# First attention of a two-layer hybrid block: heads in halves of eight on two row ranges of the array, scores and exponents issued alternately

## The chip, the cores and the metric

One core of one Trainium2 chip runs the whole program as one launch. The metric is the device time of that launch in microseconds (us), the median over several runs; lower is better.

## The reference, cut to what matters

Four batches of 512 tokens of width 512 go through attention A, a feed-forward layer, attention B and the same feed-forward layer. The change is in attention A, which has 32 heads of width 2 and a mask that keeps 51 keys for each query:

```python
sim = ...                                  # a pairwise network of 512 x 512 tokens
_, top_idx = jax.lax.top_k(sim, 51)        # mask: 0 at these, -inf elsewhere
q, k, v = heads(q), heads(k), heads(v)     # (4, 32, 512, 2)
scores = einsum('bhid,bhjd->bhij', q, k) / sqrt(2) + mask[:, None]
ao = einsum('bhij,bhjd->bhid', softmax(scores), v)
out = x + ao.reshape(B, S, 64) @ Wout.T + bout
```

## The kernel before, in words

The program runs its stages one after another on five queues (TensorE, VectorE, ScalarE, GpSimd, and SyncE for transfers). First comes the pairwise network with its top-k (`pairs`, to about 1055 us), which also projects q and k, splits each into a high and a low half for single-pass matmuls (F32R), and sends them to two stacks `qs` and `ks`. Then attention A (`attention_a`), the feed-forward layer (`feed_forward`), attention B, and the second feed-forward layer.

**The stacks.** A chunk is 16 heads of one batch; there are 8 chunks. A chunk's stack has 112 partitions: three terms (high by high, low by high, high by low) of 32 rows (16 heads by 2), and 16 rows for the negated maxima. `own_keys` is a copy of the chunk's keys in which one head is picked out: GpSimd multiplies `ks` by a column of `own_step` (L1169). It picks by differences, so that the banks need the mask only once per chunk: each further head adds its difference to what stands in PSUM.

**Steps.** `order_of_attention_a` writes out one list of steps. Each step is offered to all five queues, so the list is the order of each queue. The steps are:

- `scores` (c, h, pair): two matmuls (L998) of 128 queries by 512 keys into two of the banks 0 to 3; VectorE takes the maximum of each row over both banks at once (L1085). Banks 0, 1 and banks 2, 3 take turns. 256 steps.
- `place` (c): TensorE turns the chunk's maxima (L1006), ScalarE copies them negated (L1121), SyncE sends them into `qs` (L1185). The chunk's exponents wait for this.
- `exp` (c, keys, h, j): one matmul (L1017) of 128 keys by 512 queries into bank 4 (j = 0) or 5 (j = 1), from which ScalarE makes the exponent (L1129). The matmul waits until ScalarE has read the bank's last content: `pe.wait_ge(ex_made, i - 1)`.
- `weighted` (c, keys, group, j): exponents of four heads by their values, on four column ranges of the array (L1049). It waits for the last of the four exponents.
- At the first head of a chunk the mask is written into the banks first ("seeding"): L996 for scores, L1015 for exponents, bf16 matmuls with the identity.
- Side steps, one at most at each odd step: `turn` (mask transposed, L985), and `divide`, `feature`, `project_a` for a finished batch (L1059, L1066, L1073).
- `last_exp` (h, keys): the exponents of the last chunk, when banks 0 to 3 are free: two matmuls (L1034) and one exponent of both banks (L1135). Beside them run the first steps of the feed-forward layer (`FIRST_ROWS`): normalising rows and turning them (L1449).

`LEAD` = 36 scores steps run before the first exponent; then each exponent step (two `exp`) has one scores step beside it. One head thus needs two scores steps, two exponent steps and one `weighted`; this text calls such a pair of steps a period. TensorE meets in a period: exponent pair, scores pair, scores pair, exponent pair, `weighted`. Its queue is in order, and the wait of a matmul stands on its weight load (PEld).

Of the kernel before, what the change touches and what calls it, by code (L numbers as in the profile page):

```python
# [32 lines left out]
HALVES = 6  # L33
STACK = 16 * (HALVES + 1)

# [38 lines left out]
def build(nc, d):  # L74
    with ExitStack() as ctx:
# [38 lines left out]
        for queue in queues:  # L114
# [3 lines left out]
            queue.wait_ge(p.stacked[0], 16 * 24)  # L118
            queue.wait_ge(p.stacked[1], 16 * 24)
# [72 lines left out]
CHUNK = 16  # L192
CHUNKS = B * HA // CHUNK
LEAD, KEYS_AHEAD = 36, 1
# [44 lines left out]
def order_of_attention_a():  # L239
# [5 lines left out]
    maxima = iter([(c, h, pair) for c in range(CHUNKS) for h in range(CHUNK) for pair in range(2)])  # L245

    def next_maxima():
        for c, h, pair in [at for at in (next(maxima, None),) if at]:
            order.append(("scores", c, h, pair))
            if pair == 0 and CHUNK * c + h + KEYS_AHEAD < CHUNKS * CHUNK:  # L250
                order.append(("own_keys", CHUNK * c + h + KEYS_AHEAD))
            if (h, pair) == (CHUNK - 1, 1):
                places.append(("place", c))

    def place():

        while places and ("scores", places[0][1], CHUNK - 1, 1) not in order[-3:]:
            order.append(places.pop(0))

    for i in range(LEAD):  # L260
        next_maxima()
        place()
    for c in range(CHUNKS - 1):
        b = c // 2
        if c % 2 == 0 and b + 1 < B:
            side += [("turn", b + 1, t) for t in range(NT)]
        for i in range(2 * CHUNK):
            keys, h = divmod(i, CHUNK)
            if h % 2 == 0:
                next_maxima()  # L270
            order += [("exp", c, keys, h, 0), ("exp", c, keys, h, 1)]
            place()
            if h % 2:
                next_maxima()
            if weighted and h % 2 == 0:
                order.append(weighted.pop(0))
                if order[-1][1:] == (c - 1, 1, CHUNK // 4 - 1, 1) and c % 2 == 0:
                    side[:0] = finish_steps(b - 1)
# [4 lines left out]
            if (c % 2, i) == (0, 16) and b + 1 < B:  # L283
                order.append(("values", b + 1))
            if (c, i) == (CHUNKS - 2, 4):
                order.append(("early_root",))
    beside = iter(FIRST_ROWS)
    for h in range(CHUNK):
# [4 lines left out]
        order += next(beside, [])  # L293
        if h % 4 == 3:
            weighted += [("weighted", CHUNKS - 1, keys, h // 4, j) for keys in range(2) for j in range(2)]
# [23 lines left out]
def attention_a_memory(k, mem):  # L319
    a = Core()  # L320
    sb, signal = k.sb, k.flag
    a.ks = sb(mem, "ks", [STACK, B, 2, S])
# [2019 lines left out]
```

## Time and profile before

| | us |
|---|---|
| median of 3 runs | 3141.8 (3140.8 to 9992.69) |
| the profiled execution's own time | 3138.7 |
| its span, first to last instruction | 3137.5 |
| lead of scores alone | 1067.3 to 1116.5 |
| exponents with scores beside them | 1116.5 to 1496.8 |
| last exponents | 1496.8 to 1543.9 |
| TensorE busy / VectorE / ScalarE / GpSimd | 2981.5 / 2335.7 / 1771.8 / 1061.6 |
| mean granted TensorE clock | 0.975 |

The median and the profiled execution differ by 3.1 us. A busy time of TensorE counts the matmul's whole passage, so consecutive matmuls overlap in it; how fast they follow is read from the starts in a timeline. A row of the timeline merges like instructions: its first number is the first one's start, its second the time that they cover. "[0.21 <-ACT ex L1129]" means that the engine stood idle for 0.21 us before it, and what ended that. The clock is a share of 2.4 GHz.

### The profile page before, as it was taken

To read this page: it belongs to the slowest core of one execution; us is meant where nothing else is said; L and a number is where in the kernel's file an instruction comes from. 1 tells how busy PE (TensorE), PEld (TensorE's weight loads), DVE (VectorE), ACT (ScalarE), POOL (GpSimd) and SP (SyncE) were. 2 spreads that over 40 slices of the span, in tenths; PEclk is the share of its full clock that TensorE was granted. 3 is DMA by queue.
4 is the path that set the end of the run, shared out by engine and by line. 5 is a ranking of instruction groups with operands and counts; after the bars stand their busy time and mean duration, and the time that the engine had idled before them with its cause. 6 is when DMAs were issued, how large, how long until landed. Compare 5 with 4: busy or idle time off the path is not lost. (4 is left out here: it accounts for less than half of the span.)

```text
span 3137.5 us, 56845 instructions
## 1 busy us (share of the span) xinstructions
PE 2981.5 (95%) x22569; PEld 1795.1 (57%) x22569; DVE 2335.7 (74%) x4298; ACT 1771.8 (56%) x2897; POOL 1061.6 (34%) x881
## 2 busy tenths in 40 slices
PE   6999999999999799999899999989999987999999
PEld 3545445444556545444478778844444425887787
DVE  6998999999999877777366676655766766667665
ACT  4988888888889356666643333314443443334332
POOL 1000000000000454533255565504544554565653
PEclk9999999999999789999999999999999988999999
DMA  2000000000000000000112111143332311112111
GB/s 76 2 2 12 2 2 12 2 2 12 2 2 2 1 2 1 2 1 1 35 44 58 51 44 51 44 126 96 81 88 77 93 34 54 44 56 72 53 50 49
DMA packets 105805, 112.93 MB, mean 36 GB/s; under 512 B 8963, under 2 KB 74500, under 8 KB 105157
## 3 DMA queue, kind: packets, MB, share of 16 engines
q1 hardware_dynamic: 102918, 108.61, 12.3%
q8 instruction: 180, 2.95, 0.4%
q10 hardware_dynamic: 2624, 0.69, 0.1%
q14 instruction: 83, 0.68, 0.1%
HBM read 84.76 MB, written 20.97 MB: 34 GB/s over the span
## 5 line engine op out<-in xcount | busy, mean ns | idle before, releaser
L734 DVE TENSOR_SCALAR pair_in<-key_words,row_words 128x512 f32<-128x512 f32 x1792 | 725.8, 480 | 33.6 <-PE ps L620 29.6
L819 ACT ACTIVATE pair_mid<-ps,row_bias 128x512 f32<-128x512 f32 x896 | 589.3, 691 | 114.9 <-PE ps L620 97.4
L620 PE MATMUL ps<-pair_in,w_hi 128*32 128x512 f16 x7168 | 625.7, 390 | 11.7 <-DVE pair_in L734 11.3
L620 PE MATMUL ps<-pair_in,w_lo 128*32 128x512 f16 x3584 | 393.3, 390 | 0.0
L1085 DVE TENSOR_REDUCE maxes<-ps 128x2 f32<-128x1024 f32 x256 | 303.4, 1221 | 96.9 <-PE ps L998 95.8
L620 PEld LDWEIGHTS ps<-pair_in,w_hi 128*32 128x32 f16 x7168 | 256.1, 95 | 205.1 <-issue 37.5
L847 POOL TENSOR_SCALAR_AFFINE_SELECT sim<-sim 128x512 f32<-128x512 f32 x16 | 10.2, 641 | 1030.2 <-ACT sim L836 1030.2
L1129 ACT ACTIVATE ex<-ps 128x512 f32<-128x512 f32 x448 | 243.3, 595 | 119.0 <-PE ps L1017 118.4
L1495 PE MATMUL ps<-ffn_b_hi,ffn_a_hi 128*128 128x512 f32 x904 | 286.1, 398 | 25.1 <-DVE ffn_up L1583 9.1
L1495 PE MATMUL ps<-ffn_b_lo,ffn_a_hi 128*128 128x512 f32 x904 | 282.2, 394 | 1.7 <-DVE ffn_b_lo L1565 1.7
L1495 PE MATMUL ps<-ffn_b_hi,ffn_a_lo 128*128 128x512 f32 x904 | 281.2, 393 | 0.7 <-POOL ffn_a_lo L1726 0.7
L1633 DVE TENSOR_TENSOR x<-x,ps 128x512 f32<-128x512 f32 x256 | 175.6, 686 | 136.2 <-PE ps L1512 133.3
L635 PE MATMUL ps<-pair_mid,w_slide 128*32 128x512 f32 x2048 | 247.3, 592 | 0.0
L2240 ACT ACTIVATE ex_b<-ps 128x512 f32<-128x512 f32 x256 | 147.4, 598 | 168.4 <-PE ps L2084 162.3
L2172 DVE TENSOR_REDUCE maxes_b<-ps 128x1 f32<-128x512 f32 x256 | 169.3, 682 | 85.8 <-PE ps L2069 85.3
L1495 PEld LDWEIGHTS ps<-ffn_b_hi,ffn_a_hi 128*128 128x128 f32 x904 | 169.1, 190 | 69.6 <-DVE ffn_up L1583 11.7
L1726 POOL TENSOR_TENSOR ffn_a_lo<-ffn_sums,ffn_a_hi 128x1024 fp32r<-128x1024 f32 x60 | 148.4, 2473 | 171.0 <-ACT ffn_a_hi L1648 171.0
L1693 ACT ACTIVATE ffn_gate<-ffn_gate 128x512 f32<-128x512 f32 x60 | 37.9, 632 | 277.0 <-DVE ffn_gate L1590 277.0
L1495 PEld LDWEIGHTS ps<-ffn_b_lo,ffn_a_hi 128*128 128x128 f32 x904 | 171.4, 190 | 39.8 <-DVE ffn_b_lo L1565 3.6
L1495 PEld LDWEIGHTS ps<-ffn_b_hi,ffn_a_lo 128*128 128x128 f32 x904 | 171.4, 190 | 37.5 <-POOL ffn_a_lo L1726 1.1
L2022 POOL TENSOR_TENSOR ex_sum<-ex_sum,ex_b 128x512 f32<-128x512 f32 x124 | 156.9, 1283 | 81.9 <-ACT ex_b L2240 81.7
L620 PEld LDWEIGHTS ps<-pair_in,w_lo 128*32 128x32 f16 x3584 | 128.6, 95 | 88.2 <-issue 27.6
(240 smaller groups left out, 5434.0 us busy)
## 6 DMA issues: line engine op xcount, KB each, us to landing
ffn_raw_up<-in_w_ffn SPq DMA_DIRECT2D x64, 512.0 KB, 4.0
ffn_raw_down<-in_w_ffn SPq DMA_DIRECT2D x64, 256.0 KB, 2.7
q_stack<-halves SPq DMA_DIRECT2D x48, 256.0 KB, 5.1
k_stack<-halves SPq DMA_DIRECT2D x48, 256.0 KB, 5.9
halves<-hi_b SPq DMA_DIRECT2D x16, 512.0 KB, 2.6
halves<-lo_b SPq DMA_DIRECT2D x16, 512.0 KB, 3.6
out<-x SPq DMA_DIRECT2D x4, 1024.0 KB, 4.4
x<-in_x SPq DMA_DIRECT2D x6, 512.0 KB, 6.1
```

Source lines behind the costliest of these rows:

```text
L620: s = nc.tensor.matmul(ps[32 * quarter:32 * quarter + 32, bank + which, :], w_part[:, at_w:at_w + 32], words.rearrange("p (s two) -> p s t ...
L635: s = nc.tensor.matmul(ps[32 * c:32 * c + 32, 6 + w, :], p.w3_slide[:, 30 - 2 * r:62 - 2 * r], p.pair_mid[:, n % NG, half, :], start=r == ...
L734: s = nc.vector.tensor_scalar(p.pair_in[:, (4 * n + i) % N_PAIR, :], p.key_words[:, b % 2, :], p.row_words[:, b % 2, row:row + 1], None, A ...
L819: nc.scalar.activation(p.pair_mid[:, n % NG, which, :], ps[:, bank + which, :], ACT.Relu, bias=bias).then_inc(p.mid_made, 1)
L1085: nc.vector.tensor_reduce(maxes[:, c % 2, 2 * pair:2 * pair + 2, h], ps[:, 2 * pair:2 * pair + 2, :], AX.X, ALU.max).then_inc(maxes_made, 1)
L1129: nc.scalar.activation(ex[:, i % N_EX, :], ps[:, EXP_BANKS[j], :], ACT.Exp, scale=2.0 ** -0.5).then_inc(ex_made, 1)
L1495: i = nc.tensor.matmul(bank, a_part[:, s % 2, a_at, h, :], b_part[:, place(operand), h, :], start=opens and (which, m, h) == (0, 0, 0), st ...
L1633: nc.vector.tensor_tensor(x[:, n, :], x[:, n, :], ps[:, 6 + t % 2, :], ALU.add).then_inc(x_added, 1)
L1726: nc.gpsimd.tensor_tensor(lo, source, hi.bitcast(F32), ALU.subtract).then_inc(w_lo_made, 1)
L2022: engine.tensor_tensor(ex_sum[:, g, :], first, ex[:, i % N_EX, :], ALU.add).then_inc(done, 1)
L2172: nc.vector.tensor_reduce(maxes[:, n % 2, g, t:t + 1], ps[:, O1_BANKS[i % 3], :], AX.X, ALU.max).then_inc(max_made, 1)
L2240: nc.scalar.activation(ex[:, i % N_EX, :], ps[:, O2_BANKS[i % 2], :], ACT.Exp, scale=SCALE).then_inc(ex_made, 1)
```

## The change

A half-chunk g is now 8 heads; there are 16. A chunk's two halves lie one above the other: the even half on partitions 0 to 55 of `qs`, `ks` and `own_keys`, the odd half on 64 to 119 (48 rows of terms and 8 of maxima each). One GpSimd instruction makes the `own_keys` of a head of both halves at once, so there are 64 instead of 128. The matmuls keep their columns (128 by 512) and contract over 56 rows instead of 112. While the exponents of half g run, the scores are those of half g + 1 (12 steps of 16, on the other row range) or g + 2 (the last 4 steps, on the same row range). A step's four matmuls are issued score, exponent, score, exponent. `weighted` stands ahead of the even step instead of behind its exponents. `LEAD` is 20. The exponents kept are 24 instead of 16. Masks are seeded, and maxima placed, for each half. The last half has 16 `last_exp` steps instead of 32, and a `FIRST_ROWS` entry may follow each one instead of every second. In the pair stage the stacks take 24 transfers a batch instead of 12, and the two stacks are cleared in full at the start.

```diff
-CHUNK = 16
+CHUNK, HEADS = 16, 8
 CHUNKS = B * HA // CHUNK
-LEAD, KEYS_AHEAD = 36, 1
+HALF_CHUNKS = CHUNKS * CHUNK // HEADS
+STACK = TERMS * 2 * HEADS + HEADS
+LEAD, KEYS_AHEAD = 20, 1
...
-    for c in range(CHUNKS - 1):
+    for g in range(HALF_CHUNKS - 1):
...
-        for i in range(2 * CHUNK):
-            keys, h = divmod(i, CHUNK)
-            if h % 2 == 0:
-                next_maxima()
-            order += [("exp", c, keys, h, 0), ("exp", c, keys, h, 1)]
-            place()
-            if h % 2:
-                next_maxima()
+        for i in range(2 * HEADS):
+            keys, h = divmod(i, HEADS)
             if weighted and h % 2 == 0:
                 order.append(weighted.pop(0))
...
+            for j, scores in enumerate(next_maxima()):
+                order += scores[:1] + [("exp", g, keys, h, j)] + scores[1:]
+            place()
             if h % 4 == 3:
-                weighted += [("weighted", c, keys, h // 4, j) for j in range(2)]
+                weighted += [("weighted", c, keys, 2 * half + h // 4, j) for j in range(2)]
...
-    for h in range(CHUNK):
+    for h in range(HEADS):
         for keys in range(2):
             order.append(("last_exp", h, keys))
             if weighted:
                 order.append(weighted.pop(0))
-        order += next(beside, [])
+            order += next(beside, [])
...
+    def own_keys(n, half):
+        return own[64 * half:64 * half + STACK, n % N_KEYS, :]
+
+    def queries(g):
+        return a.qs[64 * (g % 2):64 * (g % 2) + STACK, g // 4, g // 2 % 2, :]
...
         elif kind == "exp":
-            c, keys, h, j = at
-            b, u, n, t, i = c // 2, c % 2, CHUNK * c + h, 2 * keys + j, nth_exp(*at)
-            pe.wait_ge(in_place[c % 2], 16 * (c // 2 + 1))
+            g, keys, h, j = at
+            b, n, t, i = g // 4, HEADS * (g // 2) + h, 2 * keys + j, nth_exp(*at)
+            pe.wait_ge(in_place[g % 2], 16 * (g // 2 + 1))
             pe.wait_ge(ex_made, i - 1)
...
-            nc.tensor.matmul(ps[:, EXP_BANKS[j], :], own_keys(n)[:, t * P:t * P + P], a.qs[:, b, u, :],
+            nc.tensor.matmul(ps[:, EXP_BANKS[j], :], own_keys(n, g % 2)[:, t * P:t * P + P], queries(g),
```

Before, TensorE's queue in the middle of the stage, where the exponent banks are seeded (L998 scores, L1015 seed, L1017 exponents, L1049 weighted; before.py's lines):

```order
L1017 MATMUL ps<-qs,first_keys 128x512 x2
L1049 MATMUL ps<-ex,v_aug 12x512 x4
L1017 MATMUL ps<-qs,first_keys 128x512 x2
L998 MATMUL ps<-more_keys,qs 128x512 x4
L1015 MATMUL ps<-mask_t,ident_bf 128x512
L1017 MATMUL ps<-qs,first_keys 128x512
L1015 MATMUL ps<-mask_t,ident_bf 128x512
L1017 MATMUL ps<-qs,first_keys 128x512
L1049 MATMUL ps<-ex,v_aug 12x512 x4
L1017 MATMUL ps<-qs,first_keys 128x512 x2
L998 MATMUL ps<-more_keys,qs 128x512 x4
L1017 MATMUL ps<-qs,first_keys 128x512 x2
```

Changed, TensorE at such a seeding (L1011 scores, L1029 seed, L1031 exponents, L1061 weighted; after.py's lines):

```order
L1061 MATMUL ps<-ex,v_aug 12x512 x4
L1011 MATMUL ps<-own_keys,qs 128x512
L1029 MATMUL ps<-mask_t,ident_bf 128x512
L1031 MATMUL ps<-qs,own_keys 128x512
L1011 MATMUL ps<-own_keys,qs 128x512
L1029 MATMUL ps<-mask_t,ident_bf 128x512
L1031 MATMUL ps<-qs,own_keys 128x512
L1011 MATMUL ps<-own_keys,qs 128x512
L1031 MATMUL ps<-qs,own_keys 128x512
L1011 MATMUL ps<-own_keys,qs 128x512
L1031 MATMUL ps<-qs,own_keys 128x512
L1061 MATMUL ps<-ex,v_aug 12x512 x4
```

The exponent pair that stood alone behind `weighted` now has a score ahead of each exponent, and a seed stands between a score and an exponent. In the plain periods, on the same engine, it now reads:

```order
L1061 MATMUL ps<-ex,v_aug 12x512 x4
L1011 MATMUL ps<-own_keys,qs 128x512
L1031 MATMUL ps<-qs,own_keys 128x512
L1011 MATMUL ps<-own_keys,qs 128x512
L1031 MATMUL ps<-qs,own_keys 128x512
L1011 MATMUL ps<-own_keys,qs 128x512
L1031 MATMUL ps<-qs,own_keys 128x512
L1011 MATMUL ps<-own_keys,qs 128x512
L1031 MATMUL ps<-qs,own_keys 128x512
L1061 MATMUL ps<-ex,v_aug 12x512 x4
```

The scores no longer stand together between the two exponent pairs, and `weighted` comes directly behind the odd step's second exponent and ahead of a score.

Before, TensorE's queue where the last exponents begin (L1006 turned maxima, L1030 seed, L1034 last exponents, L1449 turned rows of the feed-forward layer):

```order
L1049 MATMUL ps<-ex,v_aug 12x512 x4
L1017 MATMUL ps<-qs,more_keys 128x512 x2
L1030 MATMUL ps<-mask_t,ident_bf 128x512 x2
L1034 MATMUL ps<-qs,first_keys 128x512 x2
L1049 MATMUL ps<-ex,v_aug 12x512 x4
L1030 MATMUL ps<-mask_t,ident_bf 128x512 x2
L1034 MATMUL ps<-qs,first_keys 128x512 x2
L1049 MATMUL ps<-ex,v_aug 12x512 x4
L1034 MATMUL ps<-qs,first_keys 128x512 x8
L1449 MATMUL ps<-ident,ffn_z 128x128 x4
L1034 MATMUL ps<-qs,first_keys 128x512 x4
```

Changed, the same place (L1020, L1041, L1045, L1461 in after.py):

```order
L1020 MATMUL ps<-ident,maxes 8x128 x4
L1061 MATMUL ps<-ex,v_aug 12x512 x4
L1031 MATMUL ps<-qs,own_keys 128x512 x4
L1041 MATMUL ps<-mask_t,ident_bf 128x512 x2
L1045 MATMUL ps<-qs,own_keys 128x512 x2
L1061 MATMUL ps<-ex,v_aug 12x512 x4
L1041 MATMUL ps<-mask_t,ident_bf 128x512 x2
L1045 MATMUL ps<-qs,own_keys 128x512 x2
L1061 MATMUL ps<-ex,v_aug 12x512 x4
L1045 MATMUL ps<-qs,own_keys 128x512 x2
L1461 MATMUL ps<-ident,ffn_z 128x128 x4
```

The turned rows begin after one plain last exponent step instead of four, and from there stand behind every step.

## Rows read from the trace of the kernel before

**Rows 1.** The page, part 1: busy time, share of the span, instructions of each engine.

```profile
PE 2981.5 (95%) x22569; PEld 1795.1 (57%) x22569; DVE 2335.7 (74%) x4298; ACT 1771.8 (56%) x2897; POOL 1061.6 (34%) x881
```

**Rows 2.** Busy time by stretch, us; (x) counts instructions, PEclk is TensorE's granted clock.

```profile
1068.00:1117.00 49.00, 43.57 (x87) 19.38 (x86) 43.17 (x37) 1.87 (x2) 43.28 (x32) 0.53 0.00 1
1117.00:1491.00 374.00, 370.67 (x1926) 183.00 (x1925) 283.49 (x297) 255.37 (x479) 158.73 (x108) 1.00 0.01 1
1500.00:1510.00 10.00, 7.98 (x40) 3.58 (x32) 0.69 (x1) 9.53 (x12) 0.00 (x0) 1.00 0.37 108
```

**Rows 3.** Groups by line, 1117 to 1496.7 us (TensorE's to 1491): count | busy us, mean ns | idle before.

```profile
L1085 DVE TENSOR_REDUCE maxes<-ps 128x2 f32<-128x1024 f32 x220 | 260.6, 1221 | 88.6 <-PE ps L998 87.9
L1129 ACT ACTIVATE ex<-ps 128x512 f32<-128x512 f32 x447 | 242.8, 595 | 119.0 <-PE ps L1017 118.4
L985 PE MATMUL ps<-ident_bf,mask 128*128 128x128 bf16 x48 | 4.8, 222 | 0.0
```

**Rows 4.** Timeline, one period from 1179.69 us: start, us, engine, line, op, out<-in.

```profile
1179.69 0.30 PEld L1017 LDWEIGHTS ps<-qs,more_keys 112*128 112x128 f32 x2 [0.85 <-ACT ex L1129]
1179.69 0.73 PE L1017 MATMUL ps<-qs,more_keys 112*128 112x512 f32 x2
1180.23 1.08 ACT L1129 ACTIVATE ex<-ps 128x512 f32<-128x512 f32 x2 [0.60 <-PE ps L1017]
1180.26 1.08 PE L998 MATMUL ps<-first_keys,qs 112*128 112x512 f32 x4
1181.18 0.68 PE L1017 MATMUL ps<-qs,more_keys 112*128 112x512 f32 x2
1181.36 0.19 PEld L1017 LDWEIGHTS ps<-qs,more_keys 112*128 112x128 f32 x1 [0.22 <-ACT ex L1129]
1181.79 1.05 PE L1049 MATMUL ps<-ex,v_aug 128*12 128x512 f32 x8
1182.77 0.73 PE L1017 MATMUL ps<-qs,more_keys 112*128 112x512 f32 x2
```

**Rows 5.** Timeline, a period in which no scores are left, from 1491.78 us.

```profile
1491.78 1.05 PE L1049 MATMUL ps<-ex,v_aug 128*12 128x512 f32 x8
1493.33 0.60 PE L1006 MATMUL ps<-ident,maxes 128*16 128x128 f32 x4
1493.94 0.98 PE L1017 MATMUL ps<-qs,more_keys 112*128 112x512 f32 x2
1494.43 0.19 PEld L1017 LDWEIGHTS ps<-qs,more_keys 112*128 112x128 f32 x1 [0.30 <-ACT ex L1129]
1494.85 1.05 PE L1049 MATMUL ps<-ex,v_aug 128*12 128x512 f32 x8
```

**Rows 6.** Timeline of TensorE around 1168 us: seeding the two exponent banks.

```profile
1168.36 0.39 PE L1015 MATMUL ps<-mask_t,ident_bf 128*128 128x512 bf16 x1
1168.83 0.39 PE L1015 MATMUL ps<-mask_t,ident_bf 128*128 128x512 bf16 x1
```

**Rows 7.** Timeline of TensorE in the lead of scores alone.

```profile
1104.16 2.26 PE L998 MATMUL ps<-first_keys,qs 112*128 112x512 f32 x4 [0.34 <-DVE maxes L1085]
1106.76 2.26 PE L998 MATMUL ps<-first_keys,qs 112*128 112x512 f32 x4 [0.34 <-DVE maxes L1085]
```

**Rows 8.** Timeline of TensorE through the last exponents.

```profile
1496.77 0.60 PE L1030 MATMUL ps<-mask_t,ident_bf 128*128 128x512 bf16 x2 [0.20 <-DMA qs<-max_t]
1502.58 0.73 PE L1034 MATMUL ps<-qs,first_keys 112*128 112x512 f32 x2 [0.65 <-ACT key_rooms L1135]
1503.49 0.73 PE L1034 MATMUL ps<-qs,first_keys 112*128 112x512 f32 x2 [0.18 <-ACT key_rooms L1135]
1531.63 0.73 PE L1034 MATMUL ps<-qs,first_keys 112*128 112x512 f32 x2
1533.27 0.74 PE L1034 MATMUL ps<-qs,first_keys 112*128 112x512 f32 x2
1543.87 0.73 PE L1495 MATMUL ps<-ffn_b_hi,ffn_a_hi 128*128 128x512 f32 x2
```

More of the change, by code:

```diff
@@ L117, in build @@
             queue.wait_ge(p.x_plus_y, 2 * B)
[L118 to L119 removed]
+            queue.wait_ge(p.stacked[0], 16 * 48)
+            queue.wait_ge(p.stacked[1], 16 * 48)
             queue.wait_ge(p.qk_split, B)
@@ L244, in order_of_attention_a @@
     side, weighted, places = [], [], []
-    maxima = iter([(c, h, pair) for c in range(CHUNKS) for h in range(CHUNK) for pair in range(2)])
+    maxima = iter([(g, h, pair) for g in range(HALF_CHUNKS) for h in range(HEADS) for pair in range(2)])
     def next_maxima():
[L248 to L253, printed above, removed]
+        at = next(maxima, None)
+        if at is None:
+            return [[], []]
+        g, h, pair = at
+        keys = HEADS * (g // 2) + h + KEYS_AHEAD
+        if (h, pair) == (HEADS - 1, 1):
+            places.append(("place", g))
+        make = g % 2 == 0 and pair == 0 and keys < CHUNKS * HEADS
+        return [[("scores", *at, 0)], [("scores", *at, 1)] + [("own_keys", keys)] * make]
@@ L255, in place @@
     def place():
-        while places and ("scores", places[0][1], CHUNK - 1, 1) not in order[-3:]:
+        while places and ("scores", places[0][1], HEADS - 1, 1, 1) not in order[-5:]:
             order.append(places.pop(0))
     for i in range(LEAD):
-        next_maxima()
+        for steps in next_maxima():
+            order += steps
         place()
-    for c in range(CHUNKS - 1):
+    for g in range(HALF_CHUNKS - 1):
+        c, half = divmod(g, 2)
         b = c // 2
-        if c % 2 == 0 and b + 1 < B:
+        if g % 4 == 0 and b + 1 < B:
@@ L292, in order_of_attention_a @@
                 order.append(weighted.pop(0))
-        order += next(beside, [])
+            order += next(beside, [])
         if h % 4 == 3:
-            weighted += [("weighted", CHUNKS - 1, keys, h // 4, j) for keys in range(2) for j in range(2)]
+            weighted += [("weighted", CHUNKS - 1, keys, 2 + h // 4, j) for keys in range(2) for j in range(2)]
     assert next(beside, None) is None
@@ L527, in pairs @@
                               x_dram[b][:, 2 * half:2 * half + 2, :]).then_inc(p.x_in[b][half], 16)
-    nc.sync.dma_start(a.own_head[:, :], d["own_head"]).then_inc(a.small, 16)
+    sp.wait_ge(k.pool_setup, STACKS_EDGED)
+    for half in range(2):
+        for t in range(TERMS):
+            first = 64 * half + 2 * HEADS * t
+            nc.sync.dma_start(a.own_head[first:first + 2 * HEADS, :], d["own_head"][0:2 * HEADS, 0:HEADS]).then_inc(a.small, 16)
+        first = 64 * half + 2 * HEADS * TERMS
+        nc.sync.dma_start(a.own_head[first:first + HEADS, :], d["own_head"][96:96 + HEADS, 0:HEADS]).then_inc(a.small, 16)
     nc.sync.dma_start(a.wout_t[0:KA, :], d["wout_t"]).then_inc(a.small, 16)
@@ L1080, in vector @@
             x_rsqrt(k, a.var_made, a.sd_made, 1, EARLY_ROWS)
[L1081 to L1085 removed]
+        elif kind == "scores" and at[3]:
+            g, h, pair, i = at
+            dve.wait_ge(scores_done, 2 * (HEADS * g + h) + pair + 1)
+            dve.wait_ge(maxes_turned, g - 1)
+            nc.vector.tensor_reduce(maxes[:, g % 2, 2 * pair:2 * pair + 2, h], ps[:, 2 * pair:2 * pair + 2, :], AX.X,
                                     ALU.max).then_inc(maxes_made, 1)
```

183 lines of the change are left out of this document (87 added, 96 removed).

## The prediction

> **What bounds the kernel now.** I read the page first. TensorE is busy 2981.5 of 3137.5 us, 95%, and the other three 34 to 74% [rows 1]. That invites the thought that any matmul time taken away is gained. A share over the span says nothing of one stage, so I looked at attention A by stretches [rows 2]: in the 374 us from 1117 to 1491 TensorE is busy 370.7, VectorE 283.5, ScalarE 255.4. By groups [rows 3], the maxima cost VectorE 260.6 us and the exponents ScalarE 242.8, each with about 100 us of idle time that TensorE ends. It looks bound by TensorE. Then I read the timeline of one period [rows 4], and it says more.
>
> TensorE's side: exponent pair at 1179.69, scores from 1180.26 (four in 0.92 us, 0.23 each), exponent pair from 1181.18, weighted from 1181.79, next pair at 1182.77. The period is 3.08 us, without a gap.
>
> ScalarE's side, followed as a chain: the weight load behind weighted begins at 1179.69; the exponent begins at 1180.23, 0.54 later; two exponents take 1.08 (0.49 from the first's start to the second's, then 0.59) and end at 1181.31; 0.05 later, at 1181.36, the load of the odd step's second exponent, which had waited 0.22 for just that, begins; 0.43 later weighted begins, at 1181.79, and takes 0.98. 0.54 + 1.08 + 0.05 + 0.43 + 0.98 = 3.08. So there are two loops of the same length. TensorE's queue is full, and the two exponent banks together with weighted (during which no exponent is fed) give the same period.
>
> The proof stands near the end [rows 5]: there no scores are left. Weighted begins at 1491.78 and again at 1494.85: 3.07 us, though the 0.92 us of scores are gone and only the turned maxima stand in the gap. TensorE now waits 0.30 for ScalarE. Taking the scores off TensorE entirely leaves the period where it was. That is what the change does at its best.
>
> **Part 1, the lead.** Scores alone take 2.60 us for two steps [rows 7], bound by the maxima (2 x 1.22) [rows 3]. 16 fewer of them: -16 x 1.30 = -20.8 us.
>
> **Part 2, the last exponents.** They run from 1496.77 to 1543.87, 47.1 us for 32 steps [rows 8]. A plain step takes 0.91 (1502.58 to 1503.49), one with a weighted 1.64 (1531.63 to 1533.27). After the change: 2 seeded steps with weighted at 2.0, 4 with turned rows at about 1.05, 2 plain (1.9) and a turn (0.4), 4 with weighted of which most have a turn (7.8), 4 plain (3.7), four weighted at the end (3.6) and about 1 for the denser norm step: 26.6. That is -20.5 us; if the denser feed-forward steps get in the way it is -15.
>
> **Part 3, steps moved into the middle.** Steps with scores beside the exponents go from 224 to 240, 8 more periods: +8 x 3.07 = +24.6. Parts 1 to 3 alone give -16.7.
>
> **Part 4, a score ahead of the exponent.** Behind weighted a score's load now comes before that of the exponent. Two loads on an idle array take 0.30 together and 0.19 each, so the second begins 0.11 later [rows 4]. This lies on the exponent loop, so +0.11 x 120 = +13.2. Bounds: 0 if the loads of two row ranges go side by side; 0.23 a period, +27.6, if nothing overlaps and the score's whole matmul goes first. In 4 steps of 16 both are on the same range in any case.
>
> **Part 5, weighted moved ahead of the even step.** A group's weighted needs its fourth head's exponent, which is the step just before. Formerly an exponent pair stood between. From the load of that step's first exponent it takes 0.54 + 0.59 + 0.05 = 1.18 until weighted may start; the other way, by the second exponent's load, 0.49 + 0.43 = 0.92. So every other weighted waits about 0.27, 60 x 0.27 = 16. Behind it stands all of TensorE's queue. 24 of the side steps fall just there and cover about 0.2 each (a turn of four takes 0.4 passing and about 0.2 in sequence) [rows 3]: -4. I take +12, bounds +9 to +18.
>
> **Part 6, seeding the exponent banks.** Before, 14 events (7 chunks, two key halves), each with two seeds; a seed and its exponent take 0.47 (1168.36 to 1168.83) [rows 6], 0.24 more than an exponent's 0.23, so 0.48 an event, 6.7 us. After, 30 events. The seed uses all rows, so it stands between a score and an exponent on half the rows, and neither overlaps. The nearest row for such a switch is the pair behind weighted: 0.57 (1179.69 to 1180.26) against 0.46 for two in a run, 0.11 a switch [rows 4]. Four switches an event make 0.48 + 0.44 = 0.92, of which some falls into waiting; I take 0.8. 30 x 0.8 - 6.7 = +17.3. Bounds: +7.7 (0.48 an event) and +26.3 (1.1). The Trainium skill, TensorEngine Tiling (Array Packing), Key Properties, says that changing the tiling mode drains the engine. The 0.11 in the row agrees with it, and it speaks against this change, which puts up to four such changes beside each pair of seeds; without the rule this term would be its lower bound.
>
> **Part 7, small ones.** Seeds of the scores: 28 pairs instead of 12 in the middle, half of them in an odd step where TensorE waits for ScalarE anyway: +3 (0 to +6). Maxima placed twice as often: TensorE's part falls into the gap as in [rows 5], the transfer has four steps of lead as before: +1 (0 to +4). Keys: GpSimd does half as many; it idles for most of the stage, 0. Transfers and clearing in the pair stage lie beside 1000 us of other work: 0, at most 2.
>
> **Sum.** -20.8 - 20.5 + 24.6 + 13.2 + 12 + 17.3 + 3 + 1 = +29.8. On the execution's own 3138.7 us that is 3168.5; the median lies 3.1 higher, so I forecast 3172 us, 1% slower. A measurement of this kernel tells about 2% (63 us) from no change, so this is within it. The lowest bounds: -20.8 - 20.5 + 24.6 + 0 + 9 + 7.7 = 0, so 3142. The highest: -20.8 - 15 + 24.6 + 27.6 + 18 + 26.3 + 6 + 4 + 2 = +73, so 3215.
>
> **Rival A: TensorE is the bound, and the overlap frees it (faster).** Then the period falls to VectorE's share: 283.5 us [rows 2] over 112 periods is 2.53. 120 x 2.53 = 304, with a lead of 28.5 and an end of 26.6 it makes 359, against 476.6 now (1067.3 to 1543.9): -117; with parts 5 to 7 paid (12 + 17.3 + 4) it is -84, 3058 us. For it: a full TensorE and the idle time of the others [rows 2, 3]. Against: [rows 5]. The Trainium skill, TensorE: Matmul & The Clock Gate, section "Part 3: Packing small matmuls — row/col tiling", says that matmuls in different row groups run at the same time. No row here shows a pair on two row ranges. By that rule 0.92 of TensorE's 3.08 us goes, and if TensorE alone bounded, the result would be this rival's.
>
> **Rival B: the additions are cheap.** Loads side by side, seeds at their lower bound: the sum is near 0 to +10, 3147 us.
>
> **Rival C: the row ranges do not overlap.** Then part 4 stands at its upper bound, +14.4, and the odd step's second score delays little: 3187 us. That is the case in which the change does not do what it says. Its price is small because the exponent loop, not the sum of TensorE's work, sets the period.
>
> **Rival D: the clock (slower by more than 2%).** In the lead TensorE stood 0.34 us in every 2.6 waiting for VectorE [rows 7] and was granted 0.53, that is 1.2 GHz most of the time [rows 2]. The changed stage has more waiting. At half clock weighted takes 1.96 and the other TensorE parts of the loop about 0.6 more: a period of about 4.8, 1.5 more. It passes 2% when 22 of 120 periods run so (33 us on top of 30). Half the stage: +90, 3262 us. Against it: from 1500 to 1510 TensorE had 2 us idle in 10 and kept 1.00 [rows 2].
>
> **How the numbers follow.** Forecast 0.55, A 0.09, B 0.14, C 0.15, D 0.07. Faster by over 2% (below 3079) is most of A: 0.08. Slower by over 2% (above 3205) is D and the upper ends of the forecast and of C: 0.12. Within: 0.80. The range of 8 in 10 takes in B and C, and reaches toward A: 3112 to 3212.
>
> **What would show it.** Right: the lead about 28 us, the last exponents about 27, and between them a period of 3.1 to 3.4 us in which ScalarE is the releaser of the exponents' loads, TensorE's busy time well below its present 99%, weighted waiting for ScalarE every second time, and 1 to 2 us around each seeding. Part 4 is wrong if the exponent behind weighted starts 0.54 after weighted's end. The forecast falls if VectorE's idle time between maxima nearly goes (A), or if the clock of the stage is below 1.00 (D).

## The result, and the profile after

| | before | after |
|---|---|---|
| median, us | 3141.4 (4 runs, one of which took 9992.7) | 3199.9 (3192.7 to 3205.5, 4 runs) |
| ratio | | 1.0192, 95% interval 1.0178 to 1.0206 |
| lead of scores alone | 49.3 | 30.9 |
| middle: first exponent to first last exponent | 380.4 | 465.8 |
| last exponents, to the last `weighted` | 46.3 | 33.2 |

(Middle and end are taken here from the first exponent's start and to the last `weighted`, so 380.4 and 46.3 stand for the 380.3 and 47.1 of the table above.) The changed kernel is 1.9% slower: about 58 us, where 30 were forecast. The time is inside the range, near its upper end. The profiled execution of after took 3192.7 us, 54.0 more than that of before. The three stretches give -18.4 + 85.4 - 13.1 = +53.9, so all of it lies in attention A.

The page, part 1, of after (compare [rows 1]):

```profile
PE 3001.2 (94%) x22633; PEld 1755.6 (55%) x22665; DVE 2342.5 (73%) x4298; ACT 1779.0 (56%) x2921; POOL 960.3 (30%) x818
```

TensorE's share is 94 instead of 95%. Nobody would read a loss of 54 us out of it. Busy time by stretch of after says more (columns as in [rows 2]): lead, middle, last exponents, and 10 us within the last.

```profile
1068.20:1099.10 30.90, 27.18 (x54) 11.42 (x54) 24.02 (x20) 1.87 (x2) 24.65 (x20) 0.50 0.00 1
1099.10:1564.90 465.80, 426.89 (x2151) 157.25 (x2181) 310.85 (x317) 284.85 (x529) 77.06 (x56) 0.99 0.01 2
1564.90:1598.60 33.70, 31.39 (x148) 11.79 (x147) 8.59 (x12) 20.68 (x25) 0.00 (x0) 0.80 0.14 42
1580.00:1590.00 10.00, 10.00 (x38) 3.89 (x34) 1.12 (x2) 2.65 (x3) 0.00 (x0) 0.51 0.00 0
```

In the middle TensorE is idle for 39 us; before it was full. The overlap works, then, and nobody gains by it. The granted clock tells a little too: in after it was still 0.50 for the first 9.5 us of the middle (to 1108.6), where before it had risen to 1.00 ahead of the middle, at 1113.8. The two periods there take 4.46 and 3.42 us instead of 3.15 and 3.35, so this is some 2 of the 85 us (an estimate). Groups by line of after, in the middle (compare [rows 3]):

```profile
L1097 DVE TENSOR_REDUCE maxes<-ps 128x2 f32<-128x1024 f32 x236 | 282.4, 1223 | 146.0 <-PE ps L1011 145.2
L1141 ACT ACTIVATE ex<-ps 128x512 f32<-128x512 f32 x480 | 264.1, 595 | 179.9 <-PE ps L1031 169.1
L1031 PEld LDWEIGHTS ps<-qs,own_keys 56*128 56x128 f32 x480 | 84.6, 186 | 115.1 <-ACT ex L1141 98.3 <-issue 14.9
```

One instruction costs what it did: a maximum 1.22 us, an exponent 0.595. The waiting has grown on both: VectorE now stands 146 us and ScalarE 180 us, most of it for TensorE's results, while 98 us of the exponents' loads stand for ScalarE. Both ends of the exponent loop wait for each other. A plain period of after, timeline (columns as in [rows 4]):

```profile
1177.94 1.05 PE L1061 MATMUL ps<-ex,v_aug 128*12 128x512 f32 x8
1178.92 0.18 PEld L1011 LDWEIGHTS ps<-own_keys,qs 56*128 56x128 f32 x1 [0.85 <-DVE maxes L1097]
1178.92 0.18 PEld L1031 LDWEIGHTS ps<-qs,own_keys 56*128 56x128 f32 x1
1178.92 0.73 PE L1031 MATMUL ps<-qs,own_keys 56*128 56x512 f32 x2
1179.46 2.27 ACT L1141 ACTIVATE ex<-ps 128x512 f32<-128x512 f32 x4 [0.82 <-PE ps L1031]
1180.12 0.49 PE L1031 MATMUL ps<-qs,own_keys 56*128 56x512 f32 x1 [0.23 <-ACT ex L1141]
1180.60 0.50 PE L1031 MATMUL ps<-qs,own_keys 56*128 56x512 f32 x1
1181.29 0.12 PEld L1061 LDWEIGHTS ps<-ex,v_aug 128*12 128x12 f32 x8 [0.51 <-ACT ex L1141]
1181.29 1.05 PE L1061 MATMUL ps<-ex,v_aug 128*12 128x512 f32 x8 [0.19 <-ACT ex L1141]
```

At 1178.92 the load of a score and the load of an exponent begin together, on two row ranges. The exponent starts 0.54 us behind (1179.46), as before: nothing is lost to the score ahead of it. But `weighted` at 1181.29 has waited for ScalarE, and the period is 3.35 us instead of 3.08. The same queue right behind, where scores and exponents lie on the same row range and the score banks are seeded (L1009), up to the next `weighted` (some seeds, scores and exponents left out):

```profile
1182.27 0.61 PE L1009 MATMUL ps<-mask,ident_bf 128*128 128x512 bf16 x2
1182.81 0.50 PE L1011 MATMUL ps<-own_keys,qs 56*128 56x512 f32 x1
1183.15 0.39 PE L1031 MATMUL ps<-qs,own_keys 56*128 56x512 f32 x1
1183.38 0.39 PE L1011 MATMUL ps<-own_keys,qs 56*128 56x512 f32 x1
1183.94 0.60 PE L1020 MATMUL ps<-ident,maxes 128*8 128x128 f32 x4
1184.37 0.59 PE L1009 MATMUL ps<-mask,ident_bf 128*128 128x512 bf16 x2
...
1186.02 1.05 PE L1061 MATMUL ps<-ex,v_aug 128*12 128x512 f32 x8
```

Here everything goes in series, 0.23 us a matmul (0.34 for the one right behind seeds) and 0.54 for a pair of seeds, and the period is 4.73 us. Over a half-chunk the starts of `weighted` lie 3.35, 4.73, 3.57, 4.15, 3.52, 3.10, 3.36 and 4.08 us apart (from 1148.1 on). Before, 44 of the 110 periods lay at 3.07 to 3.10 (4 of 118 after), those with seeds mostly at 3.48, and those with seeds and turned maxima at 4.03 or more; the others have side steps. The last exponents of after, timeline of TensorE (compare [rows 8]):

```profile
1574.58 0.73 PE L1045 MATMUL ps<-qs,own_keys 56*128 56x512 f32 x2 [0.19 <-ACT ex L1147]
1576.34 1.11 PE L1461 MATMUL ps<-ident,ffn_z 128*128 128x128 f32 x4 [1.03 <-DVE ffn_z L1541]
...
1578.53 1.90 PE L1061 MATMUL ps<-ex,v_aug 128*12 128x512 f32 x8
1580.37 1.12 PE L1461 MATMUL ps<-ident,ffn_z 128*128 128x128 f32 x4
...
1590.30 1.05 PE L1061 MATMUL ps<-ex,v_aug 128*12 128x512 f32 x8
```

TensorE waits 1.03 us for the norm step, and from 1576.3 to about 1590 everything takes twice as long (`weighted` 1.84 until the next start, later 0.98): 1.2 GHz instead of 2.4.

### The profile page after: what moved, and what is told of

The parts are those of the page before. It is cut to its first block and busy times, and to the rows that moved or that the text cites. A ratio compares the mean times of both kernels' runs of the same rounds, so it can differ in the third digit from the quotient of the medians.

```text
span 3191.5 us, 56935 instructions
## 1 busy us (share of the span) xinstructions
PE 3001.2 (94%) x22633; PEld 1755.6 (55%) x22665; DVE 2342.5 (73%) x4298; ACT 1779.0 (56%) x2921; POOL 960.3 (30%) x818
## 5 line engine op out<-in xcount | busy, mean ns | idle before, releaser
L1141 ACT ACTIVATE ex<-ps 128x512 f32<-128x512 f32 x480 | 264.1, 595 | 179.9 <-PE ps L1031 169.1
L1031 PE MATMUL ps<-qs,own_keys 56*128 56x512 f32 x480 | 212.5, 466 | 32.9 <-ACT ex L1141 24.2
L1011 PE MATMUL ps<-own_keys,qs 56*128 56x512 f32 x512 | 219.9, 478 | 1.9 <-DVE maxes L1097 1.2
```

The costliest lines, as they stand in the source:

```text
L1011: s = nc.tensor.matmul(ps[:, t, :], queries(g)[:, t * P:t * P + P], own_keys(n, g % 2), start=False, stop=True, skip_group_check=True)
L1031: nc.tensor.matmul(ps[:, EXP_BANKS[j], :], own_keys(n, g % 2)[:, t * P:t * P + P], queries(g), start=False, stop=True, skip_group_check=Tr ...
L1141: nc.scalar.activation(ex[:, i % N_EX, :], ps[:, EXP_BANKS[j], :], ACT.Exp, scale=2.0 ** -0.5).then_inc(ex_made, 1)
```

## The experiments

The theory: the loop between the two exponent banks, ScalarE and `weighted` sets the period, and what the change adds to it is the loss. The first rival: TensorE's total work sets it. The others are set out with each run. Middle means the stretch of the table above. TensorE's granted clock over the middle was 1.00 before (0.996) and in run 6, 0.99 in after and in run 1, and 0.95 to 0.98 in the others; at 1.2 instead of 2.4 GHz `weighted` alone takes 1.84 us instead of 0.98. So middles that differ by a few us are compared by their periods.

**1. The kernel before with half its scores (e1).** One of the two matmuls of a scores step is left out except at each chunk's first head, and the exponents' scale is lowered so that nothing overflows: the maxima are not those of the reference.

```diff
-            for t in range(2 * pair, 2 * pair + 2):
+            for t in range(2 * pair, 2 * pair + (2 if h == 0 else 1)):
```

> The kernel before, with one of the two matmuls of every scores step left out except at a chunk's first head (its maxima are then not the reference's, so the exponents' scale is made 2^-12, which changes no duration). It takes 0.46 us of TensorE's work from each of 112 periods and nothing else. Loop theory (the two exponent banks, ScalarE and weighted set the period): the plain period stays at 3.07 to 3.08 us; only periods with side steps or seeds can gain, so the middle stage, 380 us, loses 0 to 15 us and the run takes 3125 to 3142. TensorE theory (its work is the bound): the plain period falls to 2.62 and the stage by about 50 us, 3090.

Measured: 3124.9 us (one run), lead 44.6, middle 369.4. A plain period:

```profile
1173.99 1.05 PE L1049 MATMUL ps<-ex,v_aug 128*12 128x512 f32 x8
1174.97 0.73 PE L1017 MATMUL ps<-qs,more_keys 112*128 112x512 f32 x2
1175.54 0.63 PE L998 MATMUL ps<-first_keys,qs 112*128 112x512 f32 x2
1177.08 1.05 PE L1049 MATMUL ps<-ex,v_aug 128*12 128x512 f32 x8
```

3.09 us, with 0.46 us less work for TensorE in each. The 11 us come from periods with seeds (4.03 to 3.79, 3.48 to 3.21) and with side steps (3.90 to 3.42). The loop holds; the rival, which wanted some 50 us, falls.

**2. After, with `weighted` behind the even step's exponents, as before (e2).**

```diff
-            if weighted and h % 2 == 0:
-                order.append(weighted.pop(0))
...
             for j, scores in enumerate(next_maxima()):
                 order += scores[:1] + [("exp", g, keys, h, j)] + scores[1:]
             place()
+            if weighted and h % 2 == 0:
+                order.append(weighted.pop(0))
```

> The changed kernel with weighted put back behind the even step's exponents, nothing else moved. Loop theory: every second weighted no longer waits for the exponent just issued (0.19 on TensorE and 0.25 on the weight load, at 1181.29 in the changed kernel), so the plain periods of 3.35 fall to about 3.15 and the middle stage, 465 us, by 8 to 14. If that wait costs nothing (it is only moved to the next exponent): 465 +- 3.

Measured: 3169.0 us (one run), middle 433.5 against 465.8. A plain period:

```profile
1165.35 1.05 PE L1061 MATMUL ps<-ex,v_aug 128*12 128x512 f32 x8
1166.33 0.50 PE L1011 MATMUL ps<-own_keys,qs 56*128 56x512 f32 x1
1166.33 0.50 PE L1031 MATMUL ps<-qs,own_keys 56*128 56x512 f32 x1
1168.44 1.05 PE L1061 MATMUL ps<-ex,v_aug 128*12 128x512 f32 x8
```

3.09 us again, with scores and exponents in pairs at one instant. The place of `weighted` is worth 32.3 us, nearly three times the 12 of the forecast and far outside the 8 to 14 expected. The clock does not make it: in this middle it was the lower one (0.98 against 0.99).

**3. After, with the exponent ahead of the score (e3).**

```diff
-                order += scores[:1] + [("exp", g, keys, h, j)] + scores[1:]
+                order += [("exp", g, keys, h, j)] + scores
```

> The changed kernel with each exponent ahead of its score instead of behind it. My prediction priced the score ahead of the exponent at 0.11 us a period (13 us); the trace after shows both loads starting together at 1178.92, which makes that price 0. If it is 0: the middle stage stays within 4 us of 465. If a score ahead does hold the exponent up where both are on the same row range (every fourth step, 0.23 there): 5 to 10 us less. If the prediction's price holds everywhere: 13 us less.

Measured: 3195.2 us (one run), middle 465.9, unchanged. Within it, plain periods stay (3.35), periods that seed the exponent banks fall from 4.15 to 3.72, the second one on one row range falls from 3.57 to 3.35, and those that seed the score banks rise from 4.73 to 5.23. The score ahead of the exponent costs nothing where the two lie on two row ranges. The eight periods of a half sum to 29.2 us against 29.8, some 9 us less over 15 halves (an estimate), which half clock from 1481 to 1498 and in the first periods took back: in its size the second of the three expectations holds.

**4. After, with an empty entry ahead of the turned rows that wait for the norm (e4).**

```diff
-              *([("turned", 0, f)] for f in range(ND)), [("norm", 1)], *([("turned", 1, f)] for f in range(ND)),
+              *([("turned", 0, f)] for f in range(ND)), [("norm", 1)], [], *([("turned", 1, f)] for f in range(ND)),
```

> The changed kernel with one empty entry between the second norm and the first turned row behind it, so that TensorE takes one more exponent step before it has to wait for VectorE's norm (1.03 us at 1576.34 in the changed kernel, behind which the clock was half until about 1590). If that wait is what lets the clock fall: the clock from 1564 to 1600 is 1.00 instead of 0.81 and the last exponents take 27 us instead of 34. If the clock falls for another reason (the thin work of TensorE before it): half clock again, 33 to 35 us.

Measured: 3208.1 us (3205.8 and 3210.3), ratio to before 1.0217 (1.0188 to 1.0247). TensorE does not wait 1 us there any more, and the clock is lower still:

```profile
1490.00:1500.00 10.00, 9.75 (x33) 2.88 (x33) 3.42 (x6) 2.94 (x7) 0.00 (x0) 0.50 0.00 0
1585.00:1595.00 10.00, 9.74 (x28) 5.20 (x32) 3.20 (x6) 6.06 (x7) 0.00 (x0) 0.50 0.00 0
```

The end takes 36.4 us. The first expectation failed: the clock falls without the wait for the norm. Run 3 says the same from the other side. It has that wait, and what follows runs at full speed (`weighted` takes 1.05 at 1579.02), until 1590:

```profile
1577.77 0.66 PE L1461 MATMUL ps<-ident,ffn_z 128*128 128x128 f32 x4 [1.06 <-DVE ffn_z L1541]
```

Run 4 also shows a stretch of half clock from 1489 to 1506 in the middle (475.5 us instead of 465.8), which the profiled run of after does not have. Runs 3, 5, 7, 8, 9 and 11 have one of 10 to 17 us near the same place. The same thing stands within 3 us ahead of it (in run 5 it is still under way) in all of them but run 9: TensorE waits for ScalarE, which loads another function's table for `early_root` and then that of the exponent again (1.28 us each), here in run 3, where the clock fell at 1481.0:

```profile
1480.29 0.49 PE L1031 MATMUL ps<-qs,own_keys 56*128 56x512 f32 x1 [1.58 <-ACT ex L1141]
```

This wait is 1.2 to 2.1 us long in every run. Before and runs 1, 2, 6 and 10 show only a few us of half clock behind it, after none (its wait is 1.16), run 7 with the same 1.16 shows 10 us, and in run 9 the fall comes 17 us later. So the wait goes ahead of the fall in most runs and does not settle it; what decides how long the clock stays low was not found.

**5. After, with `weighted` cut in two (e5).** Two parts of 256 queries, each between the two exponents of a step, so that exponents can be fed while it runs. `both_parts(step)` returns the step and a `weighted_rest` that takes the other half of the columns.

```diff
-                order.append(weighted.pop(0))
+                parts += both_parts(weighted.pop(0))
...
-                order += scores[:1] + [("exp", g, keys, h, j)] + scores[1:]
+                order += scores[:1] + [("exp", g, keys, h, j)]
+                if j == 0 and parts:
+                    order.append(parts.pop(0))
+                order += scores[1:]
```

> The changed kernel with each weighted cut into two instructions' groups, over the first and the last 256 queries, the first issued between the two exponents of the even step and the second between those of the odd step. TensorE's work stays the same but for one more change of tiling a period. It opens the exponent loop: one exponent is in a bank while half a weighted runs. Loop theory: the plain period falls from 3.25 on average to 2.6 to 2.8 us, the middle stage from 465 to 390 to 410, and the run to 3120 to 3150. If TensorE's work including its changes of tiling is what sets the period: at least 3.2, 3195 or slower.

Measured: 3184.7 us (3176.7 to 3199.4, 4 runs), ratio 1.0137 (1.0098 to 1.0176), middle 459.4.

```profile
1168.77 0.62 PE L1069 MATMUL ps<-ex,v_aug 128*12 128x256 f32 x8
1170.05 0.62 PE L1069 MATMUL ps<-ex,v_aug 128*12 128x256 f32 x8
1171.57 0.62 PE L1069 MATMUL ps<-ex,v_aug 128*12 128x256 f32 x8
```

The plain period is 1.28 + 1.52 = 2.80 us: below 3.08 for the first time, so the loop can be opened. The middle did not follow to the expected 390 to 410; periods with seeds became dearer (5.10 against 4.73 for the score banks), and the clock was low: 0.50 to 1125.4, the first 25 us of the middle, and 0.68 and then 0.50 from 1470 to 1490. Each costs some 7 or 8 us (an estimate from the same periods at full clock), so at full clock the middle would be about 445.

**6. The kernel before with the same cut (e6).**

```diff
-            order += [("exp", c, keys, h, 0), ("exp", c, keys, h, 1)]
+            order += [("exp", c, keys, h, 0)] + [parts.pop(0) for n in range(1) if parts] + [("exp", c, keys, h, 1)]
```

> The kernel before with weighted cut in the same way. Here TensorE has no time left (it is full at 3.08 us a period), so both theories expect no gain; the change of tiling comes twice a period. Loop theory: 3.1 to 3.35 us a period, 3140 to 3170. It tells whether the cut helps by itself, or only together with scores and exponents that overlap: a gain above 10 us here would mean that the loop, not TensorE's work, was the longer of the two.

Measured: 3172.5 us (3172.2 and 3172.8), ratio 1.0098 (1.0078 to 1.0118), middle 410.4.

```profile
1179.73 0.62 PE L1054 MATMUL ps<-ex,v_aug 128*12 128x256 f32 x8
1180.94 0.62 PE L1054 MATMUL ps<-ex,v_aug 128*12 128x256 f32 x8
1183.08 0.62 PE L1054 MATMUL ps<-ex,v_aug 128*12 128x256 f32 x8
```

A period of 1.21 + 2.14 = 3.35 us, TensorE without a gap; it is the upper end of what was expected, and the run lies 2.5 us above. Without overlap the cut only lengthens TensorE's queue. Together with runs 1 and 5 this shows the two bounds of the kernel before: taking work off TensorE leaves the period (run 1), adding to it lengthens the period (run 6), and the loop opens only where TensorE has room (run 5).

**7 and 8. After with fewer seeds: of the exponent banks (e7), of the score banks (e10).** In odd halves the mask is not written into the banks, so their scores add to what stands there; the scale of the exponents is lowered so that nothing overflows. The first change is e7's, the second e10's.

```diff
-            if h == 0:
+            if h == 0 and g % 2 == 0:
...
-            if h == 0 and i == 0:
+            if h == 0 and i == 0 and g % 2 == 0:
```

> The changed kernel with the mask written into the exponent banks only in even halves (the odd halves' exponents then stand on what the bank holds, and the exponents' scale is made 2^-12; durations are the same). It leaves out 14 or 16 of 30 seeding events of two seeds each. My prediction: 0.8 us an event, so the middle stage loses 11 to 13 us, and the periods of 4.15 in odd halves become 3.35. If seeds hide behind other waits: under 5 us.

> After, but the mask is written into the score banks only in even halves (odd halves add to what the banks hold; the scale of the exponent is 2^-12 so that nothing overflows): left out are 7 of the 14 score seedings in the middle. Prices part 7 of the sum (3 us for all score seeds, that is 0.2 per pair of seeds). The profile of after shows 4.73 us for the period with score seeds and turned maxima, against 3.36 for a plain one. If the seeds make it: these periods fall from 4.73 to about 3.6 to 3.9 in odd halves, and the middle by 7 x 1.0 = 7 us (466 to 459). If the turned maxima and the change of row range make it: they fall by 0.2 to 0.4 and the middle by 1 to 3 us.

Measured, e7: 3193.5 us (one run), middle 455.7. The starts of `weighted` around a place where the exponent banks were seeded, in after and in e7:

```profile
1159.73 1.05 PE L1061 MATMUL ps<-ex,v_aug 128*12 128x512 f32 x8 [0.20 <-ACT ex L1141]
1163.88 1.05 PE L1061 MATMUL ps<-ex,v_aug 128*12 128x512 f32 x8
```

```profile
1186.24 1.05 PE L1061 MATMUL ps<-ex,v_aug 128*12 128x512 f32 x8 [0.20 <-ACT ex L1141]
1189.38 1.05 PE L1061 MATMUL ps<-ex,v_aug 128*12 128x512 f32 x8
```

4.15 against 3.14: an event costs 1.0 us, forecast 0.8. The 14 events left out would be 14 us; the middle fell by 10, and half clock from 1472 to 1483 took the rest (three periods of 5.01, 7.18 and 4.51 us, in after 4.99, 4.44 and 3.35). Measured, e10: 3189.8 us (one run), middle 467.1. Around the place where the score banks were seeded:

```profile
1149.90 1.05 PE L1061 MATMUL ps<-ex,v_aug 128*12 128x512 f32 x8 [0.21 <-ACT ex L1141]
1153.65 1.05 PE L1061 MATMUL ps<-ex,v_aug 128*12 128x512 f32 x8
```

3.75 against 4.73 (1181.29 to 1186.02 above): 0.98 us for the two pairs of seeds of a half, forecast 0.2 a pair. The middle as a whole did not fall by 7 us; it was granted 0.97 instead of 0.99, and the periods at its start, from 1479 to 1493 and at its end are some 8 us longer than in after. So the price in the period is shown, and the 7 us of the whole are not.

**9. After, `weighted` behind, and the exponent ahead of the score at the first head of a half (e8).**

```diff
+                if h == 0:
+                    order += [("exp", g, keys, h, j)] + scores
+                else:
+                    order += scores[:1] + [("exp", g, keys, h, j)] + scores[1:]
```

> After, with weighted behind the even step's exponents (as in e2_w_behind) and, in even steps that go with the first head of a half (the ones that seed the exponent banks) and the other even steps at h = 0 only, the exponent ahead of the score. Theory (the exponent loop sets the period, parts 5 and 6 of the sum are its dearest additions): e2 left a middle of 433.5 us with 3.67 us in each period that seeds the exponent banks; exponent first took 0.4 off such a period when weighted stood ahead (e3: 4.15 to 3.72), so 29 events of 0.3 to 0.4 us: middle 422 to 426 us, the run about 3160 us. Rival (what e3 gained in those periods came from the order behind weighted, which here stands elsewhere): exponent-seed periods stay at 3.67, the middle at 433 us, the run at 3169 us.

Measured: 3159.8 us (3155.7 to 3168.2, 4 runs), ratio 1.0069 (1.0044 to 1.0094). Middle 433.5, the same as in run 2, and in halves without side steps the periods that seed the exponent banks stay at 3.68: there the rival was right. What run 3 gained in them was the same loss that run 2 had already taken away. In halves with side steps such periods did fall (4.63 to 4.11, 4.40 to 3.97), about 4 us in all, and more half clock than in run 2, from 1470 to 1480 and in the first periods, took that back. The lower time against run 2 lies in the end (30.4 us against 36.9), where the clock was 0.89 against 0.68.

**10. As 9, and `weighted` cut in two in the plain periods only (e9).**

```diff
+            whole = i in (0, 8, 12)
+            if weighted and h % 2 == 0 and not whole:
+                parts += both_parts(weighted.pop(0))
```

> As e8_c1, and weighted also cut into two halves of 256 queries, each between the two exponents of a step (as in e5_split), except in the periods that seed banks (i = 0, 8) and the one whose scores lie on the same row range (i = 12), where it stays whole behind the even step. Theory (e5's plain periods of 2.79 us open the exponent loop, and only the periods with seeds paid for it): 5 of 8 periods of a half at 2.8 instead of 3.1, which is 5 x 15 x 0.3 = 22 us off e8's middle: 400 to 405 us, the run about 3140 us, level with the kernel before (3141). Rival (a cut weighted costs four more matmuls' worth of TensorE and its queue is as full as before, so that what the plain periods give the seed periods take, as in e5): middle 420 to 430 us, the run 3155 to 3165 us.

Measured: 3157.2 us (3156.0 to 3161.9, 4 runs), ratio 1.0059 (1.0043 to 1.0075), middle 431.9. The expectation of 400 to 405 failed; the 420 to 430 of the rival is nearly met, and the first 22 us of this middle were granted 0.50, about 6 us. It is with run 9, from which its times cannot be told, the fastest variant of the changed kernel, and still slower than before.

**11. The halves on two row ranges alone, with the order of issue of the kernel before (e11).**

```diff
+            maxima_steps = [step for scores in next_maxima() for step in scores]
+            exps = [("exp", g, keys, h, j) for j in range(2)]
+            order += exps + maxima_steps if h % 2 else maxima_steps + exps
```

> The halves of eight on two row ranges are kept, the alternating issue is undone: exponent pair, scores pair, scores pair, exponent pair, weighted, as in the kernel before. Theory (the order costs, the halves by themselves only bring seeds): e8's steps whose scores and exponents lie on one row range follow in series at 0.23 us and make periods of 3.83 us, because the odd step's scores stand among the exponents; with the scores together in ScalarE's time these return to 3.1, with seeds 3.5 and 4.0. Per half 8 x 3.08 + 0.4 (seeds of keys 1) + 0.95 (first period: seeds) + 0.4 (seeds and turned maxima) = 26.4, x 15 = 396, plus some 12 for early_root and the side steps as before: middle 405 to 412 us; lead 31, end 30 to 36; the run 3132 to 3140 us, level with the kernel before (3140.5) or 0.2% ahead. Rival (the serial passage of one row range costs as such; contracting over 56 rows instead of 112 doesn't shorten it, and the seeds' switches are what costs): middle 425 to 435 us, the run 3155 to 3160 us.

Measured: 3175.9 us (3165.0 to 3176.3, 4 runs), ratio 1.0109 (1.0089 to 1.0129), middle 444.1. Both expectations failed, and usefully: with the old order the halves cost no less than in run 2, and more than the 425 to 435 of the rival (from 1460 to 1480 the clock was granted 0.66, which is some 7 us of the 444). The seeding of the exponent banks in this run:

```profile
1170.83 0.39 PE L1030 MATMUL ps<-mask_t,ident_bf 128*128 128x512 bf16 x1
1171.15 0.50 PE L1032 MATMUL ps<-qs,own_keys 56*128 56x512 f32 x1
1171.58 0.39 PE L1030 MATMUL ps<-mask_t,ident_bf 128*128 128x512 bf16 x1
1171.90 0.49 PE L1032 MATMUL ps<-qs,own_keys 56*128 56x512 f32 x1
1172.32 0.62 PE L1062 MATMUL ps<-ex,v_aug 128*12 128x512 f32 x4
```

From the first seed to the second 0.75 us, where [rows 6] show 0.47. A seed uses all 128 rows and its exponent 56; from the start of one to the start of the other it takes 0.32, and back 0.43. Before, where the exponent uses 112 rows, the matmul between the seeds of [rows 6] is:

```profile
1168.40 0.59 PE L1017 MATMUL ps<-qs,more_keys 112*128 112x512 f32 x1
```

There it is 0.04 and back 0.43. So the 0.28 us more stand, by the recorded starts, between the seed and the half-height matmul, and none on the way back. The Trainium skill, TensorEngine Tiling (Array Packing), Key Properties, says that changing the tiling mode drains the engine. These rows agree with it in one direction, full height to half height; they do not show a second price. Plain periods of this run are 3.07 us, those with seeds of exponents 3.66 and 4.06, and the two with seeds of scores and turned maxima 3.8 each or 3.3 and 4.5.

## Why the prediction was right about the direction, and where its sum fell short

The direction and the bound were right, the size was not: +54 us in the profiled execution (+58 in the median) where +30 were forecast. That the time lies in the range is partly luck, as the last paragraph of this section says. Rows 3, 6 and 7 of the table are not measured by themselves: row 3 is reckoned, and the last is what the others leave of the middle.

| term | forecast | measured |
|---|---|---|
| 1 lead | -20.8 | -18.4 |
| 2 last exponents | -20.5 | -13.1 |
| 3 eight more periods | +24.6 | +24.6 (8 times 3.08, the period where nothing is added) |
| 4 score ahead of the exponent | +13.2 | 0 (run 3, plain periods) |
| 5 `weighted` ahead of the even step | +12 | +32.3 (run 2) |
| 6 and 7 seeds, turned maxima | +21.3 | +28.5 (the rest of the middle) |
| sum | +29.8 | +53.9 |

**The reading of the bound** stood the test. A full TensorE and a full exponent loop lay one on the other; run 1 took work off TensorE and the period stayed, and after itself has a TensorE idle for 39 us in the middle. Rival A is refuted, and with it the promise that overlap pays by itself.

**Part 1** lost 2.4 us: the lead takes 30.9 and not 28.5, of which 1.8 are a wait for the transfer of the first maxima at its end (0.5 before).

**Part 2** was right in its count and wrong in its clock. Rival D held for about 14 us of the end, where it cost some 7, and for the first 9.5 us of the middle. Run 3, whose end was granted 0.94, took 28.7 us against my 26.6. That says what the end is worth when the clock nearly holds; what lets it fall is open (run 4).

**Part 4** failed at "the second begins 0.11 later". I took that from a pair of loads on one row range. On two ranges the loads start together. Its lower bound was the truth in plain periods; where seeds stand beside it or both lie on one range, the order did cost 0.6 us a half (run 3), and `weighted` behind takes that away too in halves without side steps (run 9), so that it is counted in part 5.

**Part 5** is the term that was mis-sized most, and the step is "every other weighted waits about 0.27, 60 x 0.27". For periods without seeds it is right: every second `weighted` of after shows a wait of about 0.20, and the four such periods of a half take 3.35, 3.52, 3.10 and 3.36 us against 3.08, 3.09, 3.17 and 3.09 in run 2, 0.90 more, 13.5 us over 15 halves. What the step left out are the other four, with seeds or turned maxima or on one row range: 4.73 + 3.57, 4.15 and 4.08 against 3.84 + 3.84, 3.98 and 3.67, 1.20 more, 18 us. I had priced the seeds and the place of `weighted` apart, as if one did not delay the other.

**Parts 6 and 7.** An event of exponent seeds costs 1.0 us in after (run 7). With `weighted` behind it costs 0.6 in one of a half's two events (3.67 against 3.09, run 2) and 0.9 in the other, whose period also has a step on one row range (3.98), so 0.8 lay between. The seeds of the scores were put at 3 us for all. Run 8 has 0.98 for the two pairs of a half, 13.7 us for 14 halves; before, a pair cost 0.4 (3.48 against 3.08), 4.8 for twelve. That is 8.9 more and not 3. The step that failed is "half of them in an odd step where TensorE waits for ScalarE anyway": these steps lie on one row range, everything in them goes in series, and TensorE does not wait at all (1182.27 to 1186.02 in after). Run 2's periods give an estimate of the last row of the table: 15 x (0.6 + 0.9) - 14 x 0.4 = 17 for the exponent seeds (forecast 17.3), and 14 x 1.5 - 6 x 1.35 = 13 for score seeds and turned maxima (forecast 4), together 30 against the 28.5 left over. Part 7 was mis-sized, part 6 was not.

Rival B is half right: the loads go side by side, and the additions are not cheap. Rival C named 3187 us, nearer to the measured 3199.9 than my 3172, but its cause is refuted: in 12 of 16 steps the row ranges do overlap. The range held because the misses of parts 4 and 5 have opposite signs: with the 13.2 us of part 4 on top, the time would have been 3213, just outside. That is luck.

## What to carry to other kernels

An engine at 99% can hide a second loop of just the same length. Look in the trace for a place where the engine has less to do, and see whether the period changes there; if it doesn't, freeing the engine is worth nothing by itself, and only together with a cut in the loop does the period fall (2.80 in run 5, though that run was still 1.4% slower than before). And what a finer split repeats (seeds, placing, switches between full- and half-height matmuls) is to be counted once for each repetition, with the price that it has between its new neighbours, and a wait is only taken to cover it where the new order still has that wait.

## What the runs showed of the hardware that was not expected

- Two matmuls on row ranges 0 to 55 and 64 to 119 start at the same instant, loads included (1178.92 in after, 1166.33 in run 2). Two on the same range follow at 0.23 us, whether they contract over 56 or 112 rows.
- A full-height matmul and its half-height successor take 0.75 us to the next full-height one, against 0.47 where the successor uses 112 rows. By the recorded starts the whole difference lies from full to half height, 0.32 against 0.04 (run 11, [rows 6]).
- The clock fell to 1.2 GHz in places where TensorE was far from idle (7.87 busy of the 10 us in which it fell in run 5, 8.78 of 10 at the end of after), between 1438 and 1506 and again in the last exponents, for a few us in some runs and for 10 to 41 us in others. In the middle it stood in most runs shortly behind a wait of 1.2 to 2.1 us for ScalarE's two table loads. It cost 10 us in the middle of run 4, and in run 7 it was at 0.50 for nearly the whole end, which took 43 us where run 3 took 28.7. Taking away the 1.03 us wait ahead of the fall at the end of after did not keep the clock up (run 4), and with that wait it stayed up in run 3.
